# Reordering the start of the feed-forward part of a transformer block: expert inputs before masks, wide masks on ScalarE, two output sums among the last heads

## What is computed

```
mod = (silu(c) @ wmod)                      # shift, scale and gate of both halves, per batch
h = layernorm(x) * (1 + ca) + sa
x = x + ga * attention(h)                   # 32 query heads, 8 key heads, width 64, causal
h = layernorm(x) * (1 + cb) + sb
logits = h @ gate_w.T                       # 8 experts
top_w, top_i = top_k(logits, 2); routing = softmax(top_w)
for each expert e (weight we of each row, 0 where it was not chosen):
    h1 = h @ w1.T + h @ A1[e].T @ B1[e].T * 2
    h3 = h @ w3.T + h @ A3[e].T @ B3[e].T * 2
    act = silu(h1) * h3                     # 704 columns
    out += we * (act @ w2.T + act @ A2[e].T @ B2[e].T * 2)
x = x + gb * out
```

## Time and profile before

| | us |
|---|---|
| median of 3 runs | 476.53 (476.27 to 478.54) |
| the profiled execution | 478.57 |
| its span, first to last instruction | 476.8 |
| PE busy in the span | 438.2 (92%) |
| DVE, ACT, POOL busy | 368.7, 349.5, 336.0 |
| mean granted TensorE clock | 0.981 of full speed |

### The profile page before, as it was taken

How to read it: one execution, slowest core, us unless ns; L and a number is a source line. 1 busy time by engine, 2 the same in 40 slices (tenths; PEclk the granted TensorE clock), 3 DMA queues, 4 the chain that set the end, 5 groups by cost and what they waited for, 6 DMA issues and landing times.

```text
span 476.8 us, 12257 instructions
## 1 busy us (share of the span) xinstructions
PE 438.2 (92%) x4492; PEld 315.1 (66%) x4492; DVE 368.7 (77%) x1012; ACT 349.5 (73%) x638; POOL 336.0 (70%) x276
## 2 busy tenths in 40 slices
PE   3796989999999999999999998998989997989995
PEld 3372666787878788877878786776856453545563
DVE  3588778889888889888888998988766659446477
ACT  3434899999989989889989989979816465653341
POOL 4125679999759987669999986854314885474792
PEclk9985999999999999999999999999999999999999
DMA  8226333576624375523257432364120000000001
GB/s 291 84 80 208 111 110 92 118 201 151 178 45 135 90 180 144 149 63 114 67 166 167 136 84 73 70 185 83 23 44 1 2 0 0 2 1 1 23 22 45
DMA packets 57275, 44.58 MB, mean 94 GB/s; under 512 B 36608, under 2 KB 48896, under 8 KB 57216
## 3 DMA queue, kind: packets, MB, share of 16 engines
q1 hardware_dynamic: 55728, 41.70, 32.3%
q10 hardware_dynamic: 1488, 2.10, 1.2%
HBM read 23.87 MB, written 11.53 MB: 74 GB/s over the span
## 4 chain that ended last, share of the span: by engine, by line
PE 59%; ACT 13%; DVE 12%; POOL 7%; issue 6%; DMA 1%; SPq 0%; DVEq 0%; ACTq 0%; POOLq 0%
PE ps L498 11%; PE ps L424 8%; PE ps L426 8%; PE ps L425 8%; PE ps L480 5%; PE ps L482 5%; ACT prob L883 3%; PE ps L518 3%; PE ps L522 3%; PE ps L520 3%; ACT ph L890 3%; PE ps L724 2%; PE ps L698 2%; ACT rot L862 1%; DMA wst<-chunks 1%
## 5 line engine op out<-in xcount | busy, mean ns | idle before, releaser
L1225 DVE CUSTOM_DVE_ANT_0 prob<-ps,causal 128x512 f32<-128x512 f32 (+3 forms) x256 | 117.7, 484 | 9.6 <-PE ps L482 7.8
L883 ACT ACTIVATE prob<-prob,least 128x512 f32<-128x512 f32 (+3 forms) x256 | 122.5, 555 | 0.6 <-DVE least L1225 0.6
L1233 DVE SCALAR_TENSOR_TENSOR pl<-ps,ph 128x512 f16<-128x512 f32 (+1 forms) x128 | 105.1, 821 | 20.7 <-ACT ph L890 17.0
L890 ACT ACTIVATE ph<-ps 128x512 f16<-128x512 f32 (+1 forms) x128 | 87.3, 703 | 22.8 <-PE ps L498 20.2
L480 PE MATMUL ps<-kT_h,qT 128*128 128x512 f16 (+3 forms) x256 | 76.9, 303 | 6.5 <-DMA qT<-spill 3.4
L498 PE MATMUL ps<-ident,prob 128*128 128x128 f32 x640 | 81.4, 274 | 1.3 <-DVE pl L1233 0.9
L482 PE MATMUL ps<-kT_l,qT 128*128 128x512 f16 (+3 forms) x256 | 70.6, 303 | 0.0
L498 PEld LDWEIGHTS ps<-ident,prob 128*128 128x128 f32 x640 | 68.7, 141 | 2.4 <-DVE pl L1233 1.3
L518 PE MATMUL ps<-vh,ph 128*128 128x65 f16 x640 | 64.9, 194 | 0.5 <-DVE pl L1233 0.4
L520 PE MATMUL ps<-vl,ph 128*128 128x64 f16 x640 | 64.9, 193 | 0.0
L522 PE MATMUL ps<-vh,pl 128*128 128x65 f16 x640 | 64.8, 193 | 0.0
(11 more groups left out here) (190 smaller groups left out, 1010.3 us busy)
## 6 DMA issues: line engine op xcount, KB each, us to landing
spill<-rot SPq DMA_DIRECT2D x20, 512.0 KB, 3.4
qT<-spill SPq DMA_DIRECT2D x16, 512.0 KB, 3.4
wst<-chunks SPq DMA_DIRECT2D x30, 256.0 KB, 3.7
kT_h<-spill SPq DMA_DIRECT2D x8, 256.0 KB, 3.9
oT<-wmod ACTq DMA_DIRECT2D x3, 512.0 KB, 11.5
kT_l<-spill SPq DMA_DIRECT2D x4, 256.0 KB, 5.0
raw<-chunks SPq DMA_DIRECT2D x4, 256.0 KB, 4.7
out<-xs SPq DMA_DIRECT2D x4, 256.0 KB, 2.1
```

Source lines behind the costliest of these rows:

```text
L883: act.activation(prob[:, m % 2, c], prob[:, m % 2, c], ACT.Exp, bias=least[:, m % 2, qt:qt + 1], scale=-1.0).then_inc(exp_done, 1)
L890: act.activation(ph[:, m % 2, c], ps[:, PT_BANK:PT_BANK + 3, :].rearrange("p a b -> p (a b)")[:, c], ACT.Copy, scale=PROB_SCALE).then_inc( ...
L1225: ins = dve.tensor_tensor_reduce(prob[:, m % 2, at:at + w], ps[:, bank, off:off + w], causal[:, S - w:S], -1.0 / HD ** 0.5, 3.0e38, ALU.ad ...
L1233: dve.scalar_tensor_tensor(out=pl[:, m % 2, c], in0=ps[:, PT_BANK:PT_BANK + 3, :].rearrange("p a b -> p (a b)")[:, c], scalar=PROB_SCALE, ...
```

## The change

In words:
- **PE, last heads.** Output tile (6, 2) stood behind `values(62)`; it now opens period 62, ahead of the transposes of head 63. Tile (6, 3) stood after the loop; it now stands in period 63 ahead of `values(63)`, in bank 6 (`MISC_BANK`), and waits for the logits to have been copied out of that bank.
- **DVE, last heads.** The copy of batch 0's logits (`logits_out(0)`) moves from after head 63 into period 61.
- **PE after the loop.** `lora_inputs` comes first, into banks 2 and 3 (they held transposed probabilities), then masks 0 and 1, `h_base(0, 0)`, mask 2, last outputs 0 and 1, `h_lora(0, 0)`, masks 3 and 4, last outputs 2 and 3, and `h_base(0, 1)` last. The wait for head 63's norm now stands at mask 1 alone.
- **ACT.** The three wide masks are made here by `choice_wide(0, i)` instead of by `choices_wide` on DVE. The dummy Silu with its table load now stands ahead of the first `masks_out`.
- **DVE after the loop.** `choices_difference(0)` makes the small one-hot difference (128x32) in place of the three wide instructions. The first two `op_add` of window 7 follow the four `mask_input`; the last two follow `activation_product(0, 0, 0)`.
- ACT's first `products_high` waits for all 32 output tiles, since its target shares space with `oT`.

The diff, cut:

```
             for n in range(FIRST_PERIOD, HEADS):
+                if n == HEADS - 2:
+                    pe.wait_ge(op_added, (n - 10) // 2)
+                    output(W - 1, 2, out_bank(n))
                 if 0 <= n + 1 < HEADS:
                     transpose_probs(n + 1)
+                if n == HEADS - 1:
+                    pe.wait_ge(fs["lg"], 1)
+                    output(W - 1, 3, MISC_BANK)
                 if n >= 0:
                     values(n)
...
-            pe.wait_ge(normed, HEADS)
+            lora_inputs(0, (0, 1))
+            mask_transposes(0, (0, 1))
             h_base(0, 0)
-            h_base(0, 1)
-            output(W - 1, 3, PV_BANK)
-            mask_transposes(0, (0, 1))
+            mask_transposes(0, (2,))
             last_output(0)
-            mask_transposes(0, (2,))
             last_output(1)
-            lora_inputs(0, (0, 1))
+            h_lora(0, 0)
+            mask_transposes(0, (3, 4))
             last_output(2)
             last_output(3)
-            h_lora(0, 0)
-            mask_transposes(0, (3, 4))
+            h_base(0, 1)
...
+            act.wait_ge(s_done, 3 * HEADS)
+            choice_wide(0, 0)
+            choice_wide(0, 1)
             weights_exp(0)
+            choice_wide(0, 2)
+            act.activation(c_e[:, :, :], c_sb[:, :, :], ACT.Silu)
+            masks_out(0, (0, 1))
             weights_wide(0)
-            masks_out(0, (0, 1, 2))
-            act.activation(c_e[:, :, :], c_sb[:, :, :], ACT.Silu)
-            tm_high(0)
+            tm_high(0, (0, 1))
+            masks_out(0, (2,))
+            tm_high(0, (2, 3))
...
             first_choice(0)
             second_choice(0)
-            choices_wide()
-            op_add(W - 1, 3, PV_BANK)
+            choices_difference(0)
+            op_add(W - 1, 3, MISC_BANK)
             weights(0)
-            for t in range(2):
-                op_add(W, t, MISC_BANK + t % 2)
-            mask_inputs()
-            for t in range(2, T):
-                op_add(W, t, MISC_BANK + t % 2)
+            dve.wait_ge(fs["mT"], 2)
+            mask_input(0, 0)
+            mask_input(0, 1)
+            mask_input_low(0, 0)
+            mask_input_low(0, 1)
+            dve.wait_ge(fs["mT"], 3)
+            mask_input(0, 2)
+            mask_input(0, 3)
+            op_add(W, 0, MISC_BANK + 1)
+            op_add(W, 1, MISC_BANK)
...
                     activation_product(b, f, 0)
                     if b == 0:
+                        if f == 0:
+                            op_add(W, 2, MISC_BANK + 1)
+                            op_add(W, 3, MISC_BANK)
```

More of the change, by code:

```diff
@@ L590, in _ @@
                     scores(n + 3, 0)
-                if n >= 10 and n % 2 == 0:
+                if n >= 10 and n % 2 == 0 and n < HEADS - 2:
                     if out_bank(n) == PV_BANK:
@@ L620, in mask_transposes @@
                             pe.wait_ge(fs["mT"], 5 + i)
+                    elif i == 0:
+                        pe.wait_ge(pl_ready, 2 * HEADS)
                     elif i == 1:
[L622 to L626, removed]
+                        pe.wait_ge(normed, HEADS)
+                    else:
+                        pe.wait_ge(fs["mT"], i - 1)
                     bank = 3 if b == 1 else 4 + i % 2
@@ L742, in b2_product, with last_output @@
                     mm.then_inc(fs["o_mm"], 1)
-            W = HEADS // 8 - 1
-            pe.wait_ge(normed, HEADS)
-            h_base(0, 0)
-            h_base(0, 1)
-            output(W - 1, 3, PV_BANK)
-            mask_transposes(0, (0, 1))
[L751 to L754, removed]
+            def last_output(t):
+                wait(pe, op_added, 4 * W + t - 1)
+                output(W, t, MISC_BANK + 1 - t % 2)
+            lora_inputs(0, (0, 1))
+            mask_transposes(0, (0, 1))
+            h_base(0, 0)
+            mask_transposes(0, (2,))
             last_output(0)
-            mask_transposes(0, (2,))
             last_output(1)
-            lora_inputs(0, (0, 1))
+            h_lora(0, 0)
+            mask_transposes(0, (3, 4))
             last_output(2)
             last_output(3)
-            h_lora(0, 0)
-            mask_transposes(0, (3, 4))
+            h_base(0, 1)
             for b in range(B):
@@ L915, in _, with weights_exp, choice_wide, weights_wide @@
             modulate(1, 2)
+            def weights_exp(b):
+                act.wait_ge(fs["dv"], b + 1)
+                act.activation(fs1[:, 4, :], fs1[:, 3, :], ACT.Exp).then_inc(fs["ex"], 1)
+            def choice_wide(b, i):
+                if b > 0:
+                    act.wait_ge(fs["mT_mm"], 5)
+                act.wait_ge(fs[("oh1", "oh2", "oh_d")[i]], b + 1)
+                act.activation(wide[:, i, :, :].rearrange("p t (e r) -> p t e r", r=R),
+                               fsm[:, (1, 3, 2)[i], :, :].unsqueeze(3).broadcast_to([P, T, E, R]), ACT.Copy, scale=LORA_SCALE)\
+                   .then_inc(fs["wide" if i < 2 else "dwide"], 1)
+            def weights_wide(b):
+                if b > 0:
+                    act.wait_ge(fs["mT_mm"], 5)
+                for i, name in enumerate(("w1", "w2")):
+                    act.wait_ge(fs["den"], 3 * b + 2 + i)
+                    act.activation(wide[:, 3 + i, :, :], fs1[:, 6 + i, :].unsqueeze(2).broadcast_to([P, T, P]), ACT.Copy)\
+                       .then_inc(fs[name], 1)
             def gates_wide(i):
@@ L979, in masks_out @@
                     act.activation(maskT[b][:, i, :], ps[:, bank, :], ACT.Copy).then_inc(fs["mT"], 1)
[L981 to L991, removed]
             def normalise(t):
@@ L996, in normalise @@
                                scale=rstd[:, T + t:T + t + 1]).then_inc(xn_ready, 1)
[L998 to L1004, removed]
             def products_high(i, s):
@@ L1247, in norm, with logits_out @@
                                   rsum[:, :].unsqueeze(2).broadcast_to([P, T, HD]), ALU.mult).then_inc(normed, 1)
+            def logits_out(b):
+                dve.wait_ge(fs["gate_mm"], b + 1)
+                dve.tensor_copy(fsm[:, 0, :, :].rearrange("p t e -> p (t e)"), ps[:, 6, 0:T * E]).then_inc(fs["lg"], 1)
             def op_add(w, t, bank):
@@ L1281, in _ @@
                     probs_low(n + 1, 1)
+                if n == 61:
+                    logits_out(0)
             W = HEADS // 8 - 1
@@ L1306, in first_choice @@
                 k = b + 1
-                dve.wait_ge(fs["gate_mm"], k)
-                dve.tensor_copy(one(0).rearrange("p t e -> p (t e)"), ps[:, 6, 0:T * E]).then_inc(fs["lg"], 1)
+                if b > 0:
+                    logits_out(b)
                 dve.wait_ge(fs["lg"], k)
@@ L1320, in second_choice, with choices_difference @@
                 dve.tensor_tensor(fs1[:, 3, :], fs1[:, 1, :], fs1[:, 0, :], ALU.subtract).then_inc(fs["dv"], 1)
[L1322 to L1330, removed]
+            def choices_difference(b):
+                dve.wait_ge(fs["oh2"], b + 1)
                 dve.tensor_tensor(one(2), one(3), one(1), ALU.subtract).then_inc(fs["oh_d"], 1)
```

27 lines of the change are left out of this document (11 added, 16 removed).

## The result

The changed kernel takes 474.49 us (median of 6 runs, 474.23 to 475.15) beside 476.71 us before (6 runs, 476.27 to 478.54): 2.22 us less. The ratio is 0.9941, with a 95% interval of 0.9918 to 0.9964. Measured once more beside the experiments, it came to 0.9971 (0.9955 to 0.9986). Their middles, 2.8 and 1.4 us, stand on either side of what the trace shows.

What follows compares the result with a forecast made beforehand. PE in the opening, then batch 1's chain beside it, was taken as the bound. Opening terms summed to -1.96 us, the root to -2.4; -2.2 taken from 476.53 gave 474.3 us, forecast band 474.0 to 474.9, range 473.2 to 475.7.

Steps and rivals of the forecast that it cites:

- h_second: PE's opening: h_second comes 18.5 us behind the last head, 20.45 before; tile and wait changes sum to -1.96 us.
- the root: Batch 1's chain on DVE and POOL: the root moves by -2.4 us, some 23.5 us behind the last head, 26.0 before.
- Tiles in the last heads cost nothing there: Last heads on PE: two output tiles fill idle time at no cost; the opening loses one tile, -1.31 us.
- The one-hot instruction is held by POOL to the same end: DVE's first choice: POOL's low part keeps its end at 351.37, so removing the logits' copy gains nothing.
- Rival A: DVE's choice chain: one-hot instruction not held by POOL, up to 0.9 us more gained, 473.4; chance 0.18.
- The two new waits: PE at masks 0 and 1: idle 0.97 and 0.89 us for ACT's wide masks.
- The masked chain hides with 0.2 us to spare: Operands of h_lora through ACT and DVE are ready at 359.45, 0.2 us ahead of PE at 359.66.
- drain: ACT's table load: the skill's further 1.38 us, absent in the trace; with it operands come 1.2 us late, 475.5.
- rival B: ACT's serial mask chain is late and stops PE at h_lora: 475.3, or 475.5 by the drain; chance 0.13.
- Nothing later is given back: After batch 1's root: same lists on all engines, waits move along with batch 1's logits, nothing given back or won.
- Rivals C and D: C: POOL ends slower, root 0.7 later, 477.2, chance 0.05. D: gain lost later, batch 1's choice chain, 475.6, chance 0.10.

Runs made afterwards that it cites:

- e1: Changed kernel with output tile (6, 2) back behind head 62's products and (6, 3) between expert inputs and mask 0; ratio 0.9964 to the kernel before.
- e3: Changed kernel with POOL's last low part of the heads' output waiting for the second choice; ratio 0.9985 to the kernel before.
- e5: Changed kernel with h_base(0, 0) moved ahead of masks 0 and 1 on PE; ratio 0.9951 to the kernel before.
- e2: Changed kernel with the three wide masks made on DVE again, behind the second choice, instead of on ACT; ratio 0.9967 to the kernel before.
- e9: Changed kernel with h_base(0, 0) ahead of the masks and the wide masks back on DVE; ratio 0.9941 to the kernel before.
- e11: Changed kernel with tile (6, 2) back behind head 62's products and (6, 3) between masks 0 and 1 and h_base(0, 0); ratio 0.9959 to the kernel before.
- e8: Changed kernel with POOL's first av_l held until DVE has made the second av; ratio 0.9949 to the kernel before.
- e4: Changed kernel with the dummy Silu and its table load moved behind the high parts of the first two masked inputs; ratio 0.9943 to the kernel before.
- e7: Changed kernel with h_base(0, 0) ahead of masks 0 and 1 and the dummy Silu behind the third mask copy; median 474.02 us, ratio 0.9930.
- e12: The same program as e9, run once more; ratio 0.9926 to the kernel before.

## Why the prediction was right, step by step

- **The forecast.** 474.3 us was predicted, 474.49 measured; -2.2 us against -2.22 by the medians and -2.23 by the trace. That it fits so closely is partly luck: the second comparison of the same two kernels gave 1.20 us by the medians (476.98 and 475.78). Of the two distances behind the forecast, h_second moved by 0.15 us more than its sum said and the root by 0.22 less. The prediction also took 0.5% (2.38 us) for the least that could be told from no change; the second interval tells 0.29% from it.
- **Tiles in the last heads cost nothing there.** Right. The ten transposes of head 63 follow the tile without a wait, and from the logits to the last head it is 12.47 us before and after. But the sum booked -1.31 for the tile and +0.97 and +0.89 for two waits as if they were separate. e1 shows that the tile and the waits are one item: with the tile back behind the loop the waits shrink by as much (the end differs by 0.03 us). The sum came out right because both entries were in it.
- **The one-hot instruction is held by POOL to the same end.** Right: 1.14 us in place of 0.92, same end. Rival A had no case, and e3 shows the cause by taking POOL away. This agrees with the rule that the prediction quotes from the Trainium skill.
- **The two new waits.** Predicted mask 0 at 3.56 and mask 1 at 4.91 us behind the last head; measured 3.53 and 4.82.
- **The masked chain hides with 0.2 us to spare.** The low parts ended at 358.09 (DVE, 356.80 + 1.29), 10.74 behind the last head, and PE came at 10.96. The spare was 0.2. No drain follows the table load here either: c_e starts 0.01 us behind it and the mask copy follows. So rival B didn't occur here; in e5, with PE's own waits gone, ScalarE's path did bind.
- **h_second.** Predicted 18.47 us behind the last head, measured 18.34.
- **The root.** Predicted -2.4 for the root alone, bounds -1.9 and -2.5, -2.2 taken; measured -2.18. The reason given was half right. The statistics never waited for POOL's residual sums (they ended 0.5 us before DVE's second av started; I had put their end at 20.7 us behind the last head, it was 20.1). But their end sets when the first av_l starts, and so whether it meets DVE's second av. That meeting cost 0.48 us, 1.17 in place of 0.69, which I had priced on POOL's side only. From h_second to the root it is 5.47 us with the meeting (changed kernel) and 5.00 us without it (e2, e3, e9, e11).
- **Nothing later is given back.** Right, and sharper than I had it. The prediction let PE's full stretch and batch 1's chain share the role of the bound. The column of 102.0 to 102.25 us, with e11 and e8 in it, shows that the end follows the root, and neither h_second nor the start of the statistics. Rivals C and D stayed away: the waits of the earlier trace rows are 1.20 and 1.68 us, as before.

## What to carry to other kernels

Before pricing a move, look for the wait that it would stand beside: work moved out of a stretch in which its engine waits anyway, or a wait removed ahead of another engine's serial step, wins nothing alone (e1, e5), and two edits that win 0.2 us and nothing alone can win 1 us together (e4 and e5 in e7). And find the one event from which the rest of the run has a constant length, then price every edit by what it does to that event, not by what it does to the busiest engine. Where one trace is far from the sum, look first for an event of that execution: a late landing, a fall of the granted clock (e3).

## What the runs showed of the hardware

- A DVE instruction with two SBUF operands that starts during a POOL `tensor_tensor` takes about as long as if it had waited for POOL's end. On 128x32 elements it took 0.92 and 1.14 us in place of 0.19, on 128x512 it took 1.17 in place of 0.69. Moving its start earlier left its end where it was. A reduction that starts beside the same POOL instruction (350.23 us in the profile before) kept its 0.19 us.
- An instruction with one SBUF operand (`ve`, TENSOR_SCALAR on 128x4) was held as well. Near the root it took 0.29, 0.53 or 0.81 us, and in all 14 profiles it ended 0.01 to 0.03 us behind POOL's second av_l. The same instruction at 8.01 us of the profile after, where POOL runs nothing, took 0.17 us.
- The last transposing transfer landed 4.3 us after its issue in 2 of 14 profiles (e3 and e9) and 2.5 us after it in the others. In e7 PE used it 2.9 us after its issue without a wait, so the short landing is real. e9 and e12 are the same program and differ in it. What makes the difference is open; no run here was made to tell.
- The granted TensorE clock fell in the opening of one profile of 14: in e3, from 2.4 to 1.2 GHz, when PE had taken up work again behind an idle time of 2.88 us; from 364 us on it is 1.00 again. In e9, e5 and e2, with idle times of 1.30, 1.34 and 1.96 us in the opening, it stayed at 1.00.
